# A gated block with causal attention and four experts: score contractions in two row halves, loads, a memset and table loads placed anew, another plan for the row maxima

## What is computed

```python
h = _rms(x, n1_w)
q = _rms(heads(wq), qn_w); k = _rms(heads(wk), kn_w); v = heads(wv)
scores = jnp.einsum('bhqd,bhkd->bhqk', q, k) * HD ** (-0.5)
scores = jnp.where(causal[None, None], scores, -jnp.inf)
attn = jax.nn.softmax(scores, axis=-1)
ao = jnp.einsum('bhqk,bhkd->bhqd', attn, v).transpose(0, 2, 1, 3).reshape(B, T, C) @ wo.T
ao = ao.at[:, :, :M].set(0.0)          # M = 64
x = x + ao
...
moe = wts[:, 0:1] * o0 + wts[:, 1:2] * o1 + wts[:, 2:3] * o2 + wts[:, 3:4] * o3
...
x = x + s * g                          # recurrent branch times gate, on the original x
```

## Time and profile before

| | us |
|---|---|
| median of 3 runs | 2696.18 (2693.60 to 2699.94) |
| the profiled execution | 2698.19 |
| its span | 2696.3, TensorE's mean granted clock 0.975 |
| PE busy | 2475.3 (92%) |
| DVE busy | 1936.8 (72%) |
| ACT busy | 1272.3 (47%) |
| POOL busy | 188.8 (7%) |

### The profile page before, as it was taken

One profiled execution on the slowest core, in us unless ns is written; L12 is line 12 of the kernel. 1 busy time (PEld: TensorE's weight loads), 2 busy tenths in 40 slices (PEclk: granted clock), 3 DMA queues, 4 the chain that ended last, 5 costly groups with the idle time before them and its releaser, 6 DMA issues. The chain is left out here.

```text
span 2696.3 us, 66860 instructions
## 1 busy us (share of the span) xinstructions
PE 2475.3 (92%) x26336; PEld 1758.0 (65%) x26336; DVE 1936.8 (72%) x3757; ACT 1272.3 (47%) x1940; POOL 188.8 (7%) x359
## 2 busy tenths in 40 slices
PE   5998899999888995799999999999899999999999
PEld 4777777777777775233333333333269999999998
DVE  6877777777777783798888888888546555555554
ACT  3333333433333330256666666666664444445454
POOL 0000000000000000221111011011350000000000
PEclk9999999999999997799999999999999999999999
DMA  2001000000011000311102102110220101010100
GB/s 75 14 22 30 22 22 22 22 22 22 23 26 24 23 21 20 88 36 48 56 13 60 38 27 60 30 39 13 73 66 20 39 19 39 19 39 19 39 19 28
DMA packets 138089, 90.11 MB, mean 33 GB/s; under 512 B 68544, under 2 KB 130624, under 8 KB 137856
## 3 DMA queue, kind: packets, MB, share of 16 engines
q1 hardware_dynamic: 136016, 80.55, 10.6%
q0 software_dynamic: 1840, 6.03, 0.7%
HBM read 56.89 MB, written 29.36 MB: 32 GB/s over the span
## 5 line engine op out<-in xcount | busy, mean ns | idle before, releaser
L1381 DVE TENSOR_REDUCE a_mx<-ps 128x1 f32<-128x512 f32 (+3 forms) x1120 | 702.5, 671 | 127.0 <-PE ps L1220 70.0
L1357 ACT ACTIVATE a_pt<-ps 128x1024 f32<-128x1024 f32 (+3 forms) x640 | 540.8, 896 | 350.7 <-PE ps L1240 350.2
L1260 PE MATMUL ps<-a_pt,a_v_st 128*32 128x512 f32 (+3 forms) x2560 | 300.9, 542 | 1.1 <-POOL a_pt L1178 1.0
L1938 DVE TENSOR_TENSOR e_h_lo<-v_all,e_h_hi 128x512 fp32r<-128x512 f32 x208 | 146.8, 706 | 185.6 <-ACT e_h_hi L1790 184.4
L1220 PE MATMUL ps<-arena 96*128 96x512 bf16 (+3 forms) x640 | 204.3, 361 | 16.0 <-DMA arena<-q_scratch 11.8
L1220 PE MATMUL ps<-a_ka,a_qa 96*128 96x512 bf16 (+3 forms) x640 | 198.1, 349 | 0.1
L1240 PE MATMUL ps<-arena 98*128 98x512 bf16 (+3 forms) x640 | 170.5, 350 | 19.1 <-ACT a_pt L1357 9.2
L1240 PE MATMUL ps<-a_qa,a_ka 98*128 98x512 bf16 (+3 forms) x640 | 168.1, 349 | 11.4 <-ACT a_pt L1357 10.4
L1220 PEld LDWEIGHTS ps<-arena 96*128 96x128 bf16 x640 | 62.5, 98 | 168.3 <-DVE a_mx L1381 115.7
L1788 ACT ACTIVATE v_all<-ps 128x512 f32<-128x512 f32 x176 | 103.5, 588 | 123.8 <-PE ps L1683 122.0
L1220 PEld LDWEIGHTS ps<-a_ka,a_qa 96*128 96x128 bf16 x640 | 61.6, 96 | 145.8 <-DVE a_mx L1381 100.9
(11 more groups left out here) (337 smaller groups left out, 5651.3 us busy)
## 6 DMA issues: line engine op xcount, KB each, us to landing
v_all<-o_scratch SPq DMA_DIRECT2D x256, 32.0 KB
o_scratch<-a_o_sb SPq DMA_DIRECT2D x31, 256.0 KB, 2.6
q_scratch<-r_q_part SPq DMA_DIRECT2D x192, 32.0 KB, 1.5
k_scratch<-r_k_part SPq DMA_DIRECT2D x192, 32.0 KB, 1.5
arena<-k_scratch SPq DMA_DIRECT2D x96, 64.0 KB, 2.3
arena<-q_scratch SPq DMA_DIRECT2D x96, 64.0 KB, 2.3
a_ka<-k_scratch SPq DMA_DIRECT2D x96, 64.0 KB, 2.3
a_qa<-q_scratch SPq DMA_DIRECT2D x96, 64.0 KB, 2.3
```

What stands on the lines that cost most here:

```text
L1260: last = mm(po[32 * h:32 * h + 32, off:512], v_st[b][:, j, h, :], pt[h // 2][g % 2][:, h % 2, off:512], start=(j == 0), stop=(j == 4 * qc ...
L1357: nc.scalar.activation(pt[x][g % 2][:, :, off:512], sc[x][:, :, off:512], ACT.Exp).then_inc(s_p[x], 1)
L1381: ve.tensor_reduce(mx[:, h0:h0 + heads, qt, kc:kc + 1].rearrange("p h o -> p (h o)"), pm[:, k % RING, 0:heads * width].rearrange("p (h w) ...
L1938: ve.tensor_tensor(lo[dst][:, o:o + 2, :], tmp[m % 2][:, :, :], hi[dst][:, o:o + 2, :], ALU.subtract).then_inc(s_lo.sem, s_lo.up())
```

## The change

1. *Row halves.* The six products of a head lie in two parts: four products (64 rows, `MAIN`), and two products with the two rows for the maxima (34 rows, `REST`). The heads with y = 0 use rows 0 to 63 of the array and those with y = 1 rows 64 to 127, given by `tile_position`. A score matmul of 98 rows becomes one of 64 and one of 34. A unit contracts the first part, 64 rows, in place of 96. The mask is cut into two halves of 64 rows, so a diagonal unit has two mask matmuls for each head. A diagonal unit of at most 256 columns now holds two heads of the same half; one of 128 columns held four.
2. *Loads.* A load has 24 DMAs of 16 x 2 x 512 in place of 12 of 16 x 4 x 512, and the rows of the maxima 4 in place of 2. In iteration 0 the second half of blocks 0 and 1 is issued from ACT's queue, and the loads of blocks 1, 2 and 3 have the times -9, -0.4 and 1.
3. *Plan.* A diagonal unit costs 0.2 more for each head, and the stretch of a step depends less on its width.
4. *Memset.* The memset of `wo` stands ahead of the last `cut_weights`.
5. *Table loads.* Gelu's table is loaded explicitly before turn 0, before `e2_l3` and right behind the Exp at a turn's end.
6. `cst` has 256 more columns for the masks in halves (2006 to 2262).

The core of the diff:

```diff
-F32_TABLE = [("ident", 128), ("neg_kq", 128), ("neg_qk", 128), ("ones64", 128),
+F32_TABLE = [("ident", 128), ("ident_halves", 256), ("neg_halves", 256), ("ones64", 128),
...
-PARTS_Q, PARTS_K = (0, 0, 0, 1, 1, 2), (0, 1, 2, 0, 1, 0)
-NP = 6 * AD
-NROW = NP + 2
+PARTS_Q, PARTS_K = (0, 0, 1, 1, 0, 2), (0, 1, 0, 1, 2, 0)
+MAIN = 4
+REST = 2 * AD + 2
+def rows_of(h, n):
+    return slice(64 * (h % 2), 64 * (h % 2) + n)
...
-                heads = 512 // width
-                for h in range(0, 4, heads):
+                heads = 2 if width <= 256 else 1
+                for h in range(0, 4 if heads == 1 else 2):
...
-    cost = lambda e: 0.6 if e[0] == "T" else 0.1 + e[6] * e[7] / 960
-    stretch = lambda s: 0.3 + 2.3 * step_width(s) / 512
+    cost = lambda e: 0.6 if e[0] == "T" else 0.1 + e[6] * e[7] / 960 + (0.2 * e[6] if e[2] == e[3] else 0)
+    stretch = lambda s: 1.0 + 1.5 * step_width(s) / 512
...
-                        src = io[n + "_dram"][k, b, u * 64:u * 64 + 64, tok]
-                        sp.dma_start(to[AD * r:AD * r + AD, :, :], src.rearrange("(h d) t -> d h t", d=AD)
-                                     ).then_inc(s_load[b][c], 16)
+                        src = io[n + "_dram"][k, b, u * 64:u * 64 + 64, tok].rearrange("(i y d) t -> y d i t", y=2, d=AD)
+                        for y in range(1 if it == 0 and c < 2 else 2):
+                            at_row = 64 * y + AD * (r % MAIN)
+                            sp.dma_start(to[at_row:at_row + AD, r // MAIN, :, :], src[y]).then_inc(s_load[b][c], 16)
...
-                    events.append((freed if it >= B else -10 if it == 0 else 3 + c, 0, it, c))
+                    events.append((freed if it >= B else (-10, -9, -0.4, 1)[c] if it == 0 else 3 + c, 0, it, c))
...
+                        if it == ITS - 1 and qc == 2:
+                            pool.wait_ge(s_wo_in, 16)
+                            nc.gpsimd.memset(wo[:, :, 0:MASKED], 0.0).then_inc(s_wo_masked, 1)
                         first, end = cut_at[it, qc, j]
                         cut_weights(nc, pool, io, EARLY + BETWEEN, keep["w_hi"], keep["w_lo"], stage, s_raw, s_whi, s_wlo, s_wcut,
                                     first=first, end=end)
                     if j == 4 * qc + 3 and qc == 2 and it == ITS - 1:
-                        pool.wait_ge(s_wo_in, 16)
-                        nc.gpsimd.memset(wo[:, :, 0:MASKED], 0.0).then_inc(s_wo_masked, 1)
...
+                        rows = rows_of(h0, 64)
                         for i in range(heads):
-                            at_ = width * i
-                            last = mm(out[:, at_:at_ + width], qa[b][0:NP, qc, h0 + i, 128 * (qt % 4):128 * (qt % 4) + 128],
-                                      ka[b][0:NP, h0 + i, 512 * kc:512 * kc + width], start=True, stop=kc != qc,
-                                      skip_group_check=True)
-                            if kc == qc:
-                                last = mm(out[:, at_ + width - 128:at_ + width], ident16, neg_qk, start=False, stop=True,
-                                          skip_group_check=True)
+                            last = mm(out[:, width * i:width * i + width],
+                                      qa[b][rows, 0, qc, h0 // 2 + i, 128 * (qt % 4):128 * (qt % 4) + 128],
+                                      ka[b][rows, 0, h0 // 2 + i, 512 * kc:512 * kc + width], start=True, stop=kc != qc,
+                                      tile_position=(rows.start, 0), skip_group_check=True)
+                            for half in range(2 if kc == qc else 0):
+                                last = mm(out[:, width * i + width - 128:width * i + width], cb16[rows, 0, half, :],
+                                          cb16[rows, 1, half, :], start=False, stop=half == 1,
+                                          tile_position=(rows.start, 0), skip_group_check=True)
...
-                for y in range(2):
-                    h = 2 * x + y
-                    last = mm(sc[x][:, y, off:512], ka[b][:, h, 128 * j:128 * j + 128],
-                              qa[b][:, qc, h, off:512], start=True, stop=True)
+                for part, n in enumerate((64, REST)):
+                    for y in range(2):
+                        rows = rows_of(y, n)
+                        last = mm(sc[x][:, y, off:512], ka[b][rows, part, x, 128 * j:128 * j + 128],
+                                  qa[b][rows, part, qc, x, off:512], start=part == 0, stop=part == 1,
+                                  tile_position=(rows.start, 0), skip_group_check=True)
...
+            for c in range(2):
+                tok = slice(512 * c, 512 * c + 512)
+                for to, n, parts in ((ka[0][:, :, :, tok], "k", PARTS_K), (qa[0][:, :, c, :, :], "q", PARTS_Q)):
+                    for r, k in enumerate(parts):
+                        src = io[n + "_dram"][k, 0, 0:64, tok].rearrange("(i y d) t -> y d i t", y=2, d=AD)
+                        at_row = 64 + AD * (r % MAIN)
+                        act.dma_start(to[at_row:at_row + AD, r // MAIN, :, :], src[1]).then_inc(s_load[0][c], 16)
...
-                    if more and name == "e2_l3" and o == 0:
-                        squares(t)
+                    if name == "e2_l3" and o == 0:
+                        nc.scalar.preload_act_table(ACT.Gelu)
+                        if more:
+                            squares(t)
...
                     roots(t)
                     exps(t)
+                    nc.scalar.preload_act_table(ACT.Gelu)
...
+            nc.scalar.preload_act_table(ACT.Gelu)
             turn(0, False, True)
```

More of the change, by code:

```diff
@@ L1069, in attention_phase @@
         last_unit = {e[1:3]: k for k, e in enumerate(entries) if e[0] == "U"}
-        s_load = [[sig(f"loaded{b}{c}", 1, 16 * 12).sem for c in range(QC)] for b in range(B)]
-        s_mload = [[sig(f"m_loaded{b}{c}", 1, 16 * 2).sem for c in range(QC)] for b in range(B)]
+        s_load = [[sig(f"loaded{b}{c}", 1, 16 * 24).sem for c in range(QC)] for b in range(B)]
+        s_mload = [[sig(f"m_loaded{b}{c}", 1, 16 * 4).sem for c in range(QC)] for b in range(B)]
         s_ostore = [sig(f"o_stored{c}", 1, 16).sem for c in range(QC)]
@@ L1153, in values, with ones @@
                                       ).then_inc(s_vst[b], 1)
-            nc.gpsimd.memset(ka[0][NP:NROW, :, 0:512], 1.0).then_inc(s_kones, 1)
-            pool.wait_ge(s_kones, 1)
+            def ones(b, tok):
+                for y in range(2):
+                    at_row = 64 * y + 2 * AD
+                    nc.gpsimd.memset(ka[b][at_row:at_row + 2, 1, :, tok], 1.0).then_inc(s_kones, 1)
+            ones(0, slice(0, 512))
+            pool.wait_ge(s_kones, 2)
             for b in range(B):
@@ L1161, in _ @@
             pool.wait_ge(s_vst[0], 1)
-            nc.gpsimd.memset(ka[0][NP:NROW, :, 512:T], 1.0).then_inc(s_kones, 1)
-            pool.wait_ge(s_kones, 2)
+            ones(0, slice(512, T))
+            pool.wait_ge(s_kones, 4)
             values(1)
             pool.wait_ge(s_vst[1], 1)
-            nc.gpsimd.memset(ka[1][NP:NROW, :, :], 1.0).then_inc(s_kones, 1)
-            pool.wait_ge(s_kones, 3)
+            ones(1, slice(0, T))
+            pool.wait_ge(s_kones, 6)
             pool.wait_ge(s_one, 1)
@@ L1183, in _ @@
                     if (it, qc, j) in cut_at:
-                        if it == ITS - 1:
+                        if it == ITS - 1 and qc == 1:
                             pool.wait_ge(s_pv, NS * it)
+                        if it == ITS - 1 and qc == 2:
+                            pool.wait_ge(s_wo_in, 16)
+                            nc.gpsimd.memset(wo[:, :, 0:MASKED], 0.0).then_inc(s_wo_masked, 1)
                         first, end = cut_at[it, qc, j]
@@ L1199, in _ @@
             mm = nc.tensor.matmul
-            ident16, neg_qk = (cb16[:, i, :] for i in range(2))
             def maxima(ks):
@@ L1309, in _ @@
                 if g + 1 == FIRST_STEP[1]:
[L1310 removed]
+                    pe.wait_ge(s_kones, 4)
                 if g + 1 == NS:
[L1312 removed]
+                    pe.wait_ge(s_kones, 6)
                 if g + 1 < ITS * NS:
@@ L1371, in _ @@
             ve.memset(mx[:, :, :, :], -3e38)
-            for i, name in enumerate(("ident", "neg_qk")):
-                last = ve.tensor_copy(cb16[:, i, :], const(name))
+            for i, name in enumerate(("ident_halves", "neg_halves")):
+                last = ve.tensor_copy(cb16[:, i, :, :].rearrange("p k c -> p (k c)"), const(name))
             last.then_inc(s_one, 1)
@@ L1380, in _ @@
                     _, it, qc, kc, qt, h0, heads, width = e
-                    ve.tensor_reduce(mx[:, h0:h0 + heads, qt, kc:kc + 1].rearrange("p h o -> p (h o)"),
+                    ve.tensor_reduce(mx[:, place_of(h0):place_of(h0) + heads, qt, kc],
                                      pm[:, k % RING, 0:heads * width].rearrange("p (h w) -> p h w", h=heads),
@@ L1391, in _ @@
                         before, b = divmod(it - 1, B)
```

(7 more changed lines are left out.)

26 lines of the change are left out of this document (14 added, 12 removed).

## The result

The changed kernel takes 2667.4 us in the median (four runs, 2657.44 to 2675.01) against 2696.22; the ratio is 0.9887, interval 0.9868 to 0.9906. The forecast was 2667. The profiled execution is the shortest of the four: 2657.44, span 2655.7.

The account below looks back on a forecast made before the run. PE was taken to set the attention stage's pace, DVE close behind. The terms -16.5 - 4 + 17 - 8.6 - 17.3 gave -29.4 from the profiled 2698.2, so 2668.8, less 2.0 for the median: 2667 us; range 2632 to 2690.

Parts of the forecast that it names:

- a: Attention scores and sums: no change, two half-row score matmuls overlapping to take 0.22 us.
- Rival 1: Row halves do not overlap in bf16, so slower: 2716 us at 0.25 per pair, over 2900 without overlap; chance 0.09.
- b: Full units of the maxima on PE: 96 units take 71 slots by program order, -5.4 us an iteration.
- rival 2: Half streams pack better than program order: PE -16 an iteration, held near 98 us, -53 in all, 2631; chance 0.12.
- c: Diagonal units on PE: mask matmuls in the unit's own half run one after the other, +1.0 us an iteration.
- d: What DVE leaves of PE's -4.4: 1.0 lost, net -2.5 us an iteration, -16.5 over the attention stage.
- the 101: Attention iteration time: forecast 103.6 us; under 101 or over 106 would show the prediction wrong.
- the excess of DVE: Attention steps with five full units, or a T with four: DVE exceeds PE by 3.4 us an iteration, 1.0 counted lost.
- e: First rows of the maxima at the attention start: fewer loads ahead on SP, first scores near 1093, -4 us.
- f: Third rows of the maxima, iteration 0: 96 DMAs on SP delay them, PE waits 18 to 19 us, +17.
- g: Memset ahead of the weight pieces, last iteration: PE's wait before the projection and slow matmuls behind it vanish, -8.6 us.
- h: Gelu table loaded behind the Exp at a turn's end, expert phase: 1.15 us earlier in 15 turns, -17.3.

Follow-up runs that it names:

- DVE relieved: Changed kernel with DVE's reductions of full units over the first half of the columns only; iterations 4 and 6 took 97.4 and 97.7 us, iterations 1 to 6 99.8 mean.
- the run with the split loads: Changed kernel with iteration 1's loads for blocks 2 and 3 moved behind the rows of block 2 on SP; median 2649.6 us, ratio 0.9829.

## Why the prediction was right, and where not

The time, 2667, its sign and its range held. That it held to 0.4 us is luck: two of its terms were off by about 10 and 14, in opposite directions. By its steps:

- **a (scores, no change): right.** In bf16 the halves overlap in full: four score halves take 0.43 (1513.47 to 1513.90), as two whole matmuls did in the earlier trace rows. Rival 1 is out.
- **b (full units, -5.4): too little.** The working went through an iteration in program order, so that a unit finds a partner only in a neighbour of the other half. The runs with the orders changed show streams that slip past each other, as rival 2 had it, against the rule of the Trainium skill ("TensorE: Matmul & The Clock Gate", "What overlaps and what doesn't") that was set beside it: here a later matmul of the free half started first.
- **c (diagonal units, +1.0): too much.** It counted the masks in line, 128 at 0.054 or 6.9 an iteration; without them an iteration falls by 3.1. Its sign was to be steps with diagonal units that stay near 3.0; those of 512 columns in the middle of an iteration took 3.0 to 3.3 before and take 2.6 to 2.7 now, with the plan changed too.
- **d (-2.5 an iteration): -4.8.** This is the term that was mis-sized most. With DVE relieved an iteration is 97.4, some 8.7 less than before, where b and c together had 4.4; DVE takes back 3.4 of that, where the prediction had 1.0. Rival 2 had the free packing, but its 98 was to hold with DVE at full work. So the forecast and rival 2 each held half of it. Iterations 3 and 4, at 100.9, lie just under the 101 that the prediction named as a sign of being wrong. The new plan, on which the excess of DVE was reckoned, costs 0.9 by itself. The last iteration gave -2.2 where -1.5 was forecast. Two figures beside the sum are off and do not enter it: the 16 of rival 2 comes to 14.8 by its own terms (10.4 and 4.4), and the 32 further reductions on DVE are those of all eight iterations (1152 for 1120), four in each.
- **e (-4): -3.8** at the first scores, counted from the last projection of the first phase (33.13 to 29.37), and -3.0 at the first sums; the rows go out behind four batches of loads and not eight.
- **f (+17): right in mechanism and wait**, 17.04 measured, and +20.6 by the run with the split loads. The clock behind the wait was not in the sum; 3 to 4 us went there or into the steps around it; which, no run separates. The other 1.6 of the +22.2 stay in iteration 0 also without the wait (130.8 against 129.26), where d had 0.
- **g (-8.6): -8.6.**
- **h (-17.3): -7.6.** The step that failed is "loaded at 2205.30, the table is there at 2206.6, 1.15 earlier", put whole on PE. ACT did gain 1.15 a turn. But PE's last block of the first layers still has to pass Gelu, copy and DVE's cut, 0.60, 0.63 and 0.69, while PE has other work for part of it only: a floor of 0.72 a turn, which the wait of 1.21 hit after 0.49. It was to be had from the profile: the rows of ACT and DVE behind the last block show it.

So d was 14 too small a gain, h 10 too large, f (with d's 0 for iteration 0) 5 too small a loss, and the total came out by their cancelling.

## What to carry to other kernels

Where a wait is to vanish, work out the next chain that ends at the same instruction and count only the distance to it. Where one engine's matmuls are split into row halves, reckon each half as a stream of its own, take the fuller, and then ask which engine drains the PSUM banks. A load that is "early enough anywhere" still has a place in a queue: count the issues between two transfers that someone waits for.

## What was not expected of the hardware

Matmuls of two row halves start out of program order: with the scores ordered by head, four of 64, 34, 64 and 34 rows started in pairs 0.007 us apart and took 0.45 in all. And an untouched phase of about 1060 us differed by 14 us between two executions of one and the same program (1051.98 and, on another chip, 1066.05), with granted clocks of 0.98 and 0.97 up to 1050 us; the cause is open. A single profiled span says little on a change of 0.5% here. Of the stages cut at events, iterations 1 to 7 agreed to 0.1 us between these two, iteration 0 to 0.8 and the last stretch to 0.5.
